# Embedding gathers that skip out-of-range rows, with the skipped places filled by ScalarE

## The chip, the cores and the metric

The kernel runs on one core of a Trainium2 chip. The metric is device time in microseconds (us). TensorE (PE) multiplies matrices, VectorE (DVE) and ScalarE (ACT) do elementwise work, GpSimd (POOL) here issues the gathers, and SyncE (SP) issues loads. PEld is TensorE's weight load, which runs beside its matmuls.

## The reference

A click-prediction network over 2048 samples. Each sample has 13 continuous and 26 categorical fields.

```python
cont_emb = emb_table[:CONT_FIELD][None, :, :] * conts[:, :, None]
cate_emb = emb_table[cates]                      # table: 12500 rows x 64 float32
cc = jnp.concatenate([cont_emb, cate_emb], axis=1)
pairs = jnp.einsum('bfd,bgd->bfg', cc, cc)[:, ROWS, COLS]
X = jnp.concatenate([cont_emb.reshape(B, -1), cate_emb.reshape(B, -1), pairs], axis=1)
X = relu(layernorm(X @ W1 + b1) * g + b)         # 1024 wide
X = relu(layernorm(X @ W2 + b2) * g + b)         # 1024 wide
return sigmoid(X @ Wout + bout)
```

The categories are drawn from ranges of up to about 100,000, but the table has 12,500 rows. An index at or beyond 12,500 reads the last row. In these inputs that is so for 37,651 of the 53,248 indices (71%): five fields never go beyond the table, and each of the other 21 does so in about 7 of 8 samples. So of the 128 rows of one gather 37.5 are ordinary rows on average.

## The kernel before

The batch is worked in 16 tiles of 128 samples. A tile passes through these steps:

- **Gather.** `gather(x, par)` (L474 to L485) on POOL issues 26 indirect DMAs (L481), one per categorical field. Each brings 128 rows of 256 bytes into a 64-column slice of `xb`. There is one `xb`, so tile x+1 is gathered into the places that tile x has left. The fields go in four groups, g0 to g3, of 8, 6, 6 and 6 gathers. Ahead of a group POOL waits on `trans_ready` until PE has transposed the same group of the tile before. In the loop, `progress` adds waits on older events of PE.
- **Transpose and split.** PE transposes a group (`transpose_group`, L540) into PSUM. ACT rounds it to the high part `x_hl[0]` (`split_group`, L759) and signals `ts_hi`; DVE subtracts to get the low part (L1061). Each float32 product is three matmuls (L516 to L518) of such parts.
- **Pair products.** ACT and DVE copy the parts into `g_still` and `g_move` (L765, L770, L1068). PE multiplies them in four fills, "gram 0" to "gram 3" (L583). ACT and DVE take the fills out (L800, L801, L1146, L1147), and the third fill has to wait until the first is taken.
- **First layer.** PE's order for a tile is written out by hand (`STEADY`): "own 1" to "own 3" are the transposes of groups g1 to g3 of this tile and "next 0" that of g0 of the next, with the 19 k-tiles of W1 and the four fills between them. DVE and ACT normalise the sums and store them (L748).
- **Second layer.** It starts after tile 15 and uses no gathers.

Every engine runs its instructions in the order in which they are written. In the first 90 us, W1 (some 10 MB) is loaded and split into high and low parts by ACT (L825) and DVE (L1080) beside the first two tiles. DVE turns the categories into indices in `index_chain`, which clamps them to 0 .. 12499, and copies a tile's 26 indices to `idx` two tiles ahead (`indices`, L992). One more indirect DMA (L450) brings 13 rows of 4096 bytes as padding.

Of the kernel before, what the change touches and what calls it, by code (L numbers as in the profile page):

```python
# [31 lines left out]
I32 = mybir.dt.int32  # L32
U32 = mybir.dt.uint32
ALU = mybir.AluOpType
ACT = mybir.ActivationFunctionType

P = 128
BATCH = 2048
TILES = BATCH // P
CONT = 13  # L40
CATE = 26
FIELDS = CONT + CATE
DIM = 64
VOCAB = 12500
# [22 lines left out]
GROUPS = ((0, 4), (4, 7), (7, 10), (10, 13))  # L67
NG = len(GROUPS)
# [66 lines left out]
def build(nc, conts, cates, emb, W1, b1, g1, be1, W2, b2, g2, be2, Wout, bout, rows, out):  # L135
    h1_dram = nc.dram_tensor("h1_scratch", (P, TILES, HID), F32, kind="Internal").ap()

    with ExitStack() as memory:
        def sb(name, shape, dt=F32, ctx=memory):
            return ctx.enter_context(nc.sbuf_tensor(name, shape, dt))  # L140

        def sem(name):
            return memory.enter_context(nc.semaphore(name))
# [31 lines left out]
        conts_sb = sb("conts_sb", [P, TILES * CONT])  # L175
        c1 = sb("c1", [P, CONT])
        idx_all = sb("idx_all", [P, TILES * CATE], U32)
        idx = sb("idx", [P, 2, CATE], U32)
        rows_sb = sb("rows_sb", [P, FK], U32)
        ee_bc = sb("ee_bc", [P, NN])  # L180
        ident = sb("ident", [P, P])
        small = sb("small", [P, 4 * 4])
        bn = small[:, 0:12].rearrange("p (h s) -> p h s", h=2)
        mv = small[:, 12:14]
        bout_bc = small[:, 14:15]
        st = sb("st", [P, 8])
        logit = sb("logit", [P, TILES])
        prob = sb("prob", [P, TILES])
        g1_col = sb("g1_col", [P, K2])
        be1_col = sb("be1_col", [P, K2])  # L190

# [39 lines left out]
        conts_in = sem("conts_in")  # L231
        e13_in = sem("e13_in")
        rows_in = sem("rows_in")
        idx_step = sem("idx_step")
        idx_done = sem("idx_done")
        ident_ready = sem("ident_ready")
# [73 lines left out]
        def stands_alone(eng):  # L310


            eng.sem_inc(passed, 1)

        def t_bank(g):

            return (tr[:, 0, :], gr[:, 1, :])[g % 2]
# [123 lines left out]
        @block.gpsimd  # L441
        def _(pool):
            nc.gpsimd.memset(ident[:, :], 0.0).then_inc(ident_ready, 1)
            pool.wait_ge(ident_ready, 1)
            nc.gpsimd.affine_select(out=ident[:, :], in_=ident[:, :], compare_op=ALU.not_equal, fill=1.0,
                                    base=0, pattern=[[-1, P]], channel_multiplier=1).then_inc(ident_ready, 1)

            def rows_under_zeros():

                nc.gpsimd.indirect_dma_start(  # L450
                    out=raw_lo[EK + FT][PART:PART_PAD, :], out_offset=None, in_=W1,
                    in_offset=bass.IndirectOffsetOnAxis(ap=rows_sb[0:PART_PAD - PART, 0:1], axis=0),
                ).then_inc(w1_pad, 16)

            def progress(x, f):

                if f == 7:
                    pool.wait_ge(f_trans, x - 1)
                    stands_alone(pool)
                elif f == 10:  # L460
                    pool.wait_ge(l_trans, x - 1)
                    stands_alone(pool)
                elif f == 14:
                    pool.wait_ge(trans_ready, NG * x)
                    stands_alone(pool)
                elif f in (21, 23, 25):
                    pool.wait_ge(gram_ready, FILLS * (x - 1) + (f - 19) // 2)
                    stands_alone(pool)

            def gather(x, par, first=False, tied=False):  # L470

                pool.wait_ge(idx_done, x + 1)
                stands_alone(pool)
                for g, (a, b) in enumerate(GROUPS):  # L474
                    if not first:
                        pool.wait_ge(trans_ready, NG * (x - 1) + g + 1)
                        stands_alone(pool)
                    for f in range(2 * a, 2 * b):
                        if tied:
                            progress(x, f)  # L480
                        nc.gpsimd.indirect_dma_start(  # L481
                            out=xb[:, f * DIM:(f + 1) * DIM], out_offset=None, in_=emb,
                            in_offset=bass.IndirectOffsetOnAxis(
                                ap=idx[:, par, f:f + 1], axis=0),
                        ).then_inc(gathered[g], 16)  # L485

            gather(0, 0, first=True)
            gather(1, 1)
            pool.wait_ge(rows_in, 16)
            rows_under_zeros()  # L490
            with pool.Fori(0, (TILES - 2) // 2) as i:
                for u in range(2):
                    gather(2 * i + (2 + u), u, tied=True)

            def affine2(x, par):

                pool.wait_ge(n2_ready, x + 1)
                if not isinstance(x, int) or x >= 2:
                    pool.wait_ge(logit_done, x - 1)
                nc.gpsimd.tensor_tensor(a2[par][:, :], n2[par][:, :], g2_bc, ALU.mult).then_inc(a2_mul, 1)  # L500
                pool.wait_ge(a2_mul, x + 1)
                nc.gpsimd.tensor_tensor(a2[par][:, :], a2[par][:, :], be2_bc, ALU.add).then_inc(a2_ready, 1)

            pool.wait_ge(par_in, 16 * 4)
            for x in range(2):
                affine2(x, x)
            with pool.Fori(0, (TILES - 4) // 2) as i:
                for u in range(2):
                    affine2(2 * i + (2 + u), u)
# [232 lines left out]
        def _(act):  # L742
# [5 lines left out]
                act.dma_start(h1_dram[:, at(x), :].rearrange("p o n -> p (o n)"), h1_row[:, :]).then_inc(h1_out, 16)  # L748

            act.dma_start(cates_sb, cates.rearrange("(p x) f -> p (x f)", x=TILES)).then_inc(cates_in, 16)  # L750
            act.dma_start(rows_sb[:, :], rows.bitcast(U32)).then_inc(rows_in, 16)
            act.dma_start(conts_sb[:, :], conts.rearrange("(p x) f -> p (x f)", x=TILES)).then_inc(conts_in, 16)

            def split_group(x, g):

                a, b = GROUPS[g]
                n = (b - a) * P
                act.wait_ge(trans_ready, NG * x + g + 1)
                nc.scalar.copy(x_hl[:, 0, a:b, :].rearrange("p k b -> p (k b)"), t_bank(g)[:, 0:n]).then_inc(ts_hi, 1)  # L759

            def still_copies(x, n):

# [211 lines left out]
        def _(dve):  # L974
# [23 lines left out]
            def index_chain(n, a, b, to, count=idx_step):  # L998

                f, s = cates_f[:, a:b], shift[:, a:b]  # L1000
                nc.vector.tensor_copy(f, cates_sb[:, a:b]).then_inc(idx_step, 1)
                dve.wait_ge(idx_step, n + 1)
                TS(s, f, 0.0, float(VOCAB), ALU.is_lt, ALU.mult).then_inc(idx_step, 1)
                dve.wait_ge(idx_step, n + 2)
                TT(f, f, s, ALU.add).then_inc(idx_step, 1)
                dve.wait_ge(idx_step, n + 3)
                TS(to.bitcast(I32), f, 0.0, float(VOCAB - 1), ALU.max, ALU.min).then_inc(count, 1)

            index_chain(0, 0, CATE, idx[:, 0, :], idx_done)
            index_chain(3, CATE, TILES * CATE, idx_all[:, CATE:TILES * CATE])  # L1010
            indices(1, 1)
            step(nc.vector.memset(parts[:, 128:192], 0.0))
            step(nc.vector.memset(vbd[:, :, :], 0.0))
            step(nc.vector.memset(ones, 1.0))
# [389 lines left out]
```

## Time and profile before

| | us |
|---|---|
| median of 3 runs | 801.86 |
| lowest and highest | 799.72, 802.04 |
| span of the profiled execution | 797.8 |
| median less that span | 4.1 |
| PE busy | 742.0 |
| DVE busy | 552.8 |
| ACT busy | 501.8 |
| POOL busy | 492.0 |

The profile gives the span from the first to the last instruction of one execution; a time of that execution by the clock of the runs isn't given, so the difference between the median and the span stands for what lies around it. The engines overlap, so busy times don't add up. The share of a busy time says little alone: POOL has nothing to issue in the second layer, so its gathers all lie in the first 560 us.

### The profile page before, as it was taken

The numbers are of one execution on the slowest core, as the hardware profiler recorded it, in microseconds if no ns is written. First come the engines' busy times: TensorE is split into PE (matmuls) and PEld (weight loads), VectorE is DVE, ScalarE is ACT, GpSimd is POOL, SyncE is SP. The second block draws the span as 40 slices with busy tenths as digits, with TensorE's granted clock in tenths as the row PEclk, the third lists the DMA queues.
The fourth block names the chain that finished last, engine by engine and source line by source line (L and its number), as shares of the span: only waits on it lengthen the run. The fifth ranks groups of instructions, "written<-read, shape, count | busy, mean of one in ns | idle before, by whom it ended". The sixth has DMA issues, their size and how long they took to land. (4 is left out here: it accounts for less than half of the span.)

```text
span 797.8 us, 11844 instructions
## 1 busy us (share of the span) xinstructions
PE 742.0 (93%) x3583; PEld 596.2 (75%) x3583; DVE 552.8 (69%) x1703; ACT 501.8 (63%) x878; POOL 492.0 (62%) x451
## 2 busy tenths in 40 slices
PE   5678889999999999999999999999799999999995
PEld 1446668787787877878788777787678888888884
DVE  7248677787776867777677776777577555665568
ACT  2386767777577775877757777686667455355451
POOL 6776777777777777777777777777000334334432
PEclk9889999999999999999999999999899999999998
DMA  9999584766748677485775867657465111011000
GB/s 278 185 172 119 36 52 25 54 49 29 50 27 53 48 28 50 26 53 49 28 49 26 49 53 27 48 27 51 103 199 205 28 53 53 26 53 53 26 1 1
DMA packets 26232, 50.69 MB, mean 64 GB/s; under 512 B 10413, under 2 KB 10669, under 8 KB 26208
## 3 DMA queue, kind: packets, MB, share of 16 engines
q0 software_dynamic: 13344, 13.71, 43.3%
q1 hardware_dynamic: 10128, 27.97, 10.8%
q10 hardware_dynamic: 2736, 8.71, 2.7%
q8 instruction: 12, 0.20, 0.1%
q14 instruction: 12, 0.10, 0.0%
HBM read 41.96 MB, written 8.40 MB: 63 GB/s over the span
## 5 line engine op out<-in xcount | busy, mean ns | idle before, releaser
L481 POOL DMA_INDIRECT xb<-in_L_rec_emb_table,idx x416 | 423.4, 1018 | 133.3 <-issue 124.6
L516 PE MATMUL acc<-w_hi,x_hl 128*128 128x512 f32 x416 | 176.1, 423 | 6.0 <-DVE x_hl L1061 4.0
L518 PE MATMUL acc<-w_hi,x_hl 128*128 128x512 f32 x416 | 166.7, 401 | 0.0
L517 PE MATMUL acc<-w_lo,x_hl 128*128 128x512 f32 x416 | 165.8, 399 | 0.0
L500 POOL TENSOR_TENSOR raw_lo<-raw_lo,raw_hi 128x1024 f32<-128x1024 f32 x14 | 33.4, 2388 | 154.9 <-ACT raw_lo L947 154.9
L770 ACT CAST g_move<-x_hl 64x384 fp32r<-64x384 f32 (+1 forms) x192 | 125.7, 655 | 2.8
L765 ACT CAST g_still<-x_hl 64x384 fp32r<-64x384 f32 (+1 forms) x96 | 100.6, 1048 | 1.9
L516 PE MATMUL acc<-w_hi 128*128 128x512 f32 x256 | 101.0, 394 | 0.0
L518 PE MATMUL acc<-w_hi,w_lo 128*128 128x512 f32 x256 | 99.9, 390 | 0.0
L516 PEld LDWEIGHTS acc<-w_hi,x_hl 128*128 128x128 f32 x416 | 80.7, 194 | 25.5 <-DVE x_hl L1061 5.7
L517 PE MATMUL acc<-w_lo,w_hi 128*128 128x512 f32 x256 | 99.7, 390 | 0.0
L518 PEld LDWEIGHTS acc<-w_hi,x_hl 128*128 128x128 f32 x416 | 80.0, 192 | 18.4
L517 PEld LDWEIGHTS acc<-w_lo,x_hl 128*128 128x128 f32 x416 | 80.9, 195 | 12.5
L516 PE MATMUL acc<-w_hi,f_slots 128*128 128x512 f32 x192 | 77.8, 405 | 4.2 <-DVE w_lo L1080 3.7
L518 PE MATMUL acc<-w_hi,f_slots 128*128 128x512 f32 x192 | 75.8, 395 | 0.0
L517 PE MATMUL acc<-w_lo,f_slots 128*128 128x512 f32 x192 | 75.5, 393 | 0.0
L1301 DVE TENSOR_TENSOR w_lo<-raw_lo,w_hi 128x256 fp32r<-128x256 f32 x64 | 34.6, 555 | 50.8 <-ACT w_hi L939 50.7
L1068 DVE TENSOR_SCALAR g_still<-x_hl 64x384 fp32r<-64x384 f32 (+1 forms) x96 | 66.0, 687 | 1.9
L1061 DVE TENSOR_TENSOR x_hl<-tr,x_hl 128x512 fp32r<-128x512 f32 (+1 forms) x32 | 20.0, 624 | 54.7 <-ACT x_hl L759 54.7
L518 PEld LDWEIGHTS acc<-w_hi,w_lo 128*128 128x128 f32 x256 | 48.1, 188 | 10.0
L516 PEld LDWEIGHTS acc<-w_hi 128*128 128x128 f32 x256 | 48.1, 188 | 9.5
L517 PEld LDWEIGHTS acc<-w_lo,w_hi 128*128 128x128 f32 x256 | 48.2, 188 | 9.4
(117 smaller groups left out, 1171.1 us busy)
## 6 DMA issues: line engine op xcount, KB each, us to landing
raw_lo<-in_L_rec_W SPq DMA_DIRECT2D x26, 512.0 KB, 9.4
h_scratch<-h_row ACTq DMA_DIRECT2D x16, 512.0 KB, 4.8
raw_hi<-h_scratch SPq DMA_DIRECT2D x16, 512.0 KB, 3.6
xb<-in_L_rec_emb_table,idx POOLq DMA_INDIRECT x416, 6.3
raw_hi<-in_L_rec_W SPq DMA_DIRECT2D x6, 512.0 KB, 7.2
raw_hi<-in_L_rec_b SPq DMA_DIRECT2D x1, 512.0 KB, 3.8
raw_hi<-in_L_rec_ln_g SPq DMA_DIRECT2D x1, 512.0 KB, 4.7
raw_hi<-in_L_rec_ln_b SPq DMA_DIRECT2D x1, 512.0 KB, 5.5
```

Source lines behind the costliest of these rows:

```text
L481: nc.gpsimd.indirect_dma_start(out=xb[:, f * DIM:(f + 1) * DIM], out_offset=None, in_=emb, in_offset=bass.IndirectOffsetOnAxis(ap=idx[:, p ...
L500: nc.gpsimd.tensor_tensor(a2[par][:, :], n2[par][:, :], g2_bc, ALU.mult).then_inc(a2_mul, 1)
L516: nc.tensor.matmul(o, a, w, start=first, stop=False)
L517: nc.tensor.matmul(o, a, v, start=False, stop=False)
L518: return nc.tensor.matmul(o, b, w, start=False, stop=last)
L765: nc.scalar.copy(*still_part(0, n, of))
L770: last = nc.scalar.copy(*move_part(n, m // 2, m % 2))
L1061: TT(x_hl[:, 1, a:b, :].rearrange("p k b -> p (k b)"), t_bank(g)[:, 0:n], x_hl[:, 0, a:b, :].rearrange("p k b -> p (k b)").bitcast(F32), A ...
L1068: last = TS(to, x_lo.bitcast(F32), 2.0, None, ALU.mult)
L1301: TT(y_lo[:, par, part, :], y[:, part, :], y_hi[:, par, part, :].bitcast(F32), ALU.subtract).then_inc(y_split, 1)
```

## The change

DVE clamps the indices to 12500 in place of 12499, so an index beyond the table becomes 12500. Each gather gets `bounds_check=VOCAB - 1` (12499) and `oob_is_err=False`: rows with an index above that are not to be written. What then stands in their place has been put there before: ACT copies the table's last row, which it has loaded once with 128 copies (`last_row`), over the whole place of a group (`fill`). It does so for all four groups at the start, and after that for group g right behind the rounding copy of group g, when the transpose has read the place. POOL now waits on `filled` in place of `trans_ready`. The first gather too waits on it.

To make room, `idx` becomes the first 52 columns of `idx_all` (so the copy of tile 1's indices goes), and `logit` and `prob` use `conts_sb`.

```diff
-        idx = sb("idx", [P, 2, CATE], U32)
+        idx = idx_all[:, 0:2 * CATE].rearrange("p (x f) -> p x f", x=2)
+        last_row = sb("last_row", [P, DIM])
-        logit = sb("logit", [P, TILES])
-        prob = sb("prob", [P, TILES])
+        logit, prob = conts_sb[:, 0:TILES], conts_sb[:, TILES:2 * TILES]
...
                 for g, (a, b) in enumerate(GROUPS):
-                    if not first:
-                        pool.wait_ge(trans_ready, NG * (x - 1) + g + 1)
-                        stands_alone(pool)
+                    pool.wait_ge(filled, NG * x + g + 1)
+                    stands_alone(pool)
...
                                 ap=idx[:, par, f:f + 1], axis=0),
+                            bounds_check=VOCAB - 1, oob_is_err=False,
                         ).then_inc(gathered[g], 16)
...
             act.dma_start(cates_sb, cates.rearrange("(p x) f -> p (x f)", x=TILES)).then_inc(cates_in, 16)
+            act.dma_start(last_row[:, :], emb[VOCAB - 1:VOCAB, :].to_broadcast([P, DIM])).then_inc(last_row_in, 16)
             act.dma_start(rows_sb[:, :], rows.bitcast(U32)).then_inc(rows_in, 16)
...
-            def split_group(x, g):
+            def fill(g):
+
+                a, b = GROUPS[g]
+                to = xb[:, 2 * a * DIM:2 * b * DIM].rearrange("p (f d) -> p f d", d=DIM)
+                nc.scalar.copy(to, last_row[:, :].unsqueeze(1).to_broadcast([P, 2 * (b - a), DIM])).then_inc(filled, 1)
+
+            def split_group(x, g, last=False):
...
                 nc.scalar.copy(x_hl[:, 0, a:b, :].rearrange("p k b -> p (k b)"), t_bank(g)[:, 0:n]).then_inc(ts_hi, 1)
+                if not last:
+                    fill(g)
+
+            act.wait_ge(last_row_in, 16)
+            for g in range(NG):
+                fill(g)
...
-                TS(to.bitcast(I32), f, 0.0, float(VOCAB - 1), ALU.max, ALU.min).then_inc(count, 1)
+                TS(to.bitcast(I32), f, 0.0, float(VOCAB), ALU.max, ALU.min).then_inc(count, 1)
...
-            indices(1, 1)
+            dve.wait_ge(idx_step, 7)
+            dve.sem_inc(idx_done, 1)
```

No call passes `last=True`, so tile 15's groups are followed by a fill too. On ACT, in the loop over the tiles, the stretch from g2's rounding copy (`x_hl<-tr`) to g3's (`x_hl<-gr`) reads like this before:

```order
L759 CAST x_hl<-tr 128x384
L787 CAST f_slots<-gr 128x384
L770 COPY g_move<-x_hl 64x7x128
L792 CAST f_slots<-gr 59x128
L770 COPY g_move<-x_hl 64x7x128
L758 REGISTER_ALU
L759 CAST x_hl<-gr 128x384
```

and like this after, on the same engine at the same place:

```order
L768 CAST x_hl<-tr 128x384
L761 COPY xb<-last_row 128x384
L802 CAST f_slots<-gr 128x384
L785 COPY g_move<-x_hl 64x7x128
L807 CAST f_slots<-gr 59x128
L785 COPY g_move<-x_hl 64x7x128
L767 REGISTER_ALU
L768 CAST x_hl<-gr 128x384
L761 COPY xb<-last_row 128x384
```

A fill stands behind each rounding copy, so everything that ACT does after it for the tile comes one fill later. At the start of ACT's program, ahead of W1's first rounding copy, stand now one more load and four fills:

```order
L752 DMA spare<-in_r_cates 128x416
L753 DMA last_row<-in_L_rec_emb_table 128x64
L754 DMA rows_sb<-feature_rows 128x1
L755 DMA conts_sb<-in_r_conts 128x208
L761 ACT_TABLE_LOAD
L761 COPY xb<-last_row 128x512
L761 COPY xb<-last_row 128x384 x3
L840 CAST w_hi<-raw_lo 128x1024 x4
```

The order of POOL's gathers and of PE's and DVE's work is as before.

## Rows read from the trace of the kernel before

**Rows 1.** The page: busy us, share of the span, instructions.
```profile
span 797.8 us, 11844 instructions
...
PE 742.0 (93%) x3583; PEld 596.2 (75%) x3583; DVE 552.8 (69%) x1703; ACT 501.8 (63%) x878; POOL 492.0 (62%) x451
```

**Rows 2.** The gathers' line L481: durations, POOL's idle time ahead of them, landing.
```profile
L481 POOL DMA_INDIRECT xb<-in_L_rec_emb_table,idx x416: 940/944/4307, 5.0 to 558.5; - x139
...
  issue: 124.6, 398
...
DMA to landing us min/median/max: 4.8/6.3/13.6
```

**Rows 3.** The page, part 5: count | busy, mean ns | idle before.
```profile
L481 POOL DMA_INDIRECT xb<-in_L_rec_emb_table,idx x416 | 423.4, 1018 | 133.3 <-issue 124.6
```

**Rows 4.** Timeline, POOL: start us, us, instruction [idle before]: first gather, three places, last.
```profile
5.02 1.32 POOL L481 DMA_INDIRECT xb<-in_L_rec_emb_table,idx  x1 [3.54 <-DVE idx L1007]
...
163.32 1.64 POOL L481 DMA_INDIRECT xb<-in_L_rec_emb_table,idx  x1 [0.30 <-issue]
...
186.50 0.95 POOL L481 DMA_INDIRECT xb<-in_L_rec_emb_table,idx  x1 [0.30 <-issue]
...
536.99 1.15 POOL L481 DMA_INDIRECT xb<-in_L_rec_emb_table,idx  x1 [0.30 <-issue]
...
558.49 0.94 POOL L481 DMA_INDIRECT xb<-in_L_rec_emb_table,idx  x1 [0.30 <-issue]
```

**Rows 5.** Timeline, PE: transposes of groups of tiles 4 to 7, then the last.
```profile
180.20 0.63 PE L540 MATMUL tr<-ident,xb 128*128 128x128 f32 x4 [0.33 <-DVE cc_dots L1147]
...
193.43 0.49 PE L540 MATMUL gr<-ident,xb 128*128 128x128 f32 x3
...
279.53 0.63 PE L540 MATMUL tr<-ident,xb 128*128 128x128 f32 x4 [0.32 <-DVE cc_dots L1147]
...
566.58 0.90 PE L540 MATMUL gr<-ident,xb 128*128 128x128 f32 x3 [4.28 <-DMA xb<-in_L_rec_emb_table,idx]
```

**Rows 6.** Waits from 100 to 570 us: total us, times, longest.
```profile
PEld gr L583 <- ACT cc_dots L801: 9.1, 14, 2.2
PE gr L540 <- DMA xb<-in_L_rec_emb_table,idx: 8.1, 5, 4.3
```

**Rows 7.** Timeline, POOL: its shortest instruction, its compare-and-select, and the padding gather.
```profile
0.25 0.10 POOL L1392 MEMSET const-float32-0.0<- 128x1 f32 x1 [0.25 <-issue]
...
1.19 0.29 POOL L445 TENSOR_SCALAR_AFFINE_SELECT ident<-ident 128x128 f32<-128x128 f32 x1 [0.24 <-POOL ident L443]
...
81.92 0.89 POOL L450 DMA_INDIRECT raw_lo<-in_L_rec_W,rows_sb  x1 [0.30 <-issue]
```

**Rows 8.** Timeline, ACT: tile 4 from g0's rounding copy to g3's.
```profile
180.87 0.59 ACT L759 CAST x_hl<-tr 128x512 fp32r<-128x512 f32 x1 [0.82 <-PE tr L540]
...
184.26 0.48 ACT L759 CAST x_hl<-gr 128x384 fp32r<-128x384 f32 x1 [2.80 <-PE gr L540]
184.77 3.69 ACT L765 CAST g_still<-x_hl 64x896 fp32r<-64x896 f32 x2
188.70 0.48 ACT L782 CAST f_slots<-tr 128x384 fp32r<-128x384 f32 x1 [0.24 <-PE tr L554]
...
194.08 0.48 ACT L759 CAST x_hl<-gr 128x384 fp32r<-128x384 f32 x1
```

**Rows 9.** Source L770, ACT's copies of 64x384 and 64x896: durations in ns.
```profile
L770 ACT CAST g_move<-x_hl x192: 507/513/947, 41.6 to 574.4; 64x384 fp32r<-64x384 f32 x128, 64x896 fp32r<-64x896 f32 x64
```

**Rows 10.** DMA from 20 to 60 us: share of the 16 engines by queue; landing.
```profile
q0 software_dynamic: 839, 0.87, 51.9%
q1 hardware_dynamic: 1717, 6.24, 46.4%
...
xb<-in_L_rec_emb_table,idx POOLq DMA_INDIRECT x29, 11.5
```

**Rows 11.** Windows: stretch, its us, busy (x instructions) of PE, PEld, DVE, ACT, POOL.
```profile
0.00:80.00 80.00, 56.38 (x193) 34.11 (x194) 46.46 (x132) 41.57 (x57) 57.23 (x58) 0.89 0.96 188
```

More of the change, by code:

```diff
@@ L233, in build @@
         rows_in = sem("rows_in")
+        last_row_in = sem("last_row_in")
+        filled = sem("filled")
         idx_step = sem("idx_step")
```

## The prediction

> **What bounds the kernel now.** I read the busy times first [rows 1]. PE is busy for 742.0 of 797.8 us, so it looks like the bound, with 56 us idle. POOL, at 62%, looks like an engine with room. The reader should not stop there. I then took the gathers' own line [rows 2, 3]: 416 gathers are busy for 423.4 us, and POOL is idle for 133.3 us ahead of them, of which 124.6 us is "issue", in 398 pieces of 0.31 us. That is time in which POOL waits for no other engine. So POOL runs one gather after another without a pause from 5.02 to 559.4 us [rows 4]: 423.4 + 133.3 + 5.0, less the 3.5 us of idle time ahead of the first, plus 1.2 for the padding gather, is 559.4. A usual gather takes 0.944 us and its gap 0.31, so 1.25 us, or 32.6 us for a tile's 26.
>
> The third thing to see is that this stream and PE are nearly equal in speed. From the first gather of g1 of tile 4 at 163.32 to that of tile 15 at 536.99 is 373.7 us for 11 tiles, 33.97 us each [rows 4]. PE, left alone, needs less: from the g0 transpose at 180.20 to that at 279.53 it does 3 tiles in 33.1 us each [rows 5]. The difference first eats up a lead: tile 4's last group is transposed at 193.43 without waiting. Later PE waits for the rows themselves, 8.1 us in five pieces, the last of 4.28 us at 566.58 [rows 5, 6]. So the first 567 us are set by the gather stream, with PE's own chain less than 1 us per tile behind it. What follows, 797.8 - 566.6 = 231 us, has no gathers, and I take it as unchanged. A nanosecond more per gather is then 0.42 us of the end. That is the most important number here.
>
> **The change, part by part.**
>
> The gather instruction itself. It gets a comparison for each of its 128 indices and some way to leave rows out. No row of the trace shows a gather with such a bound, so its price has to be bounded from both sides.
> Below: 71% of the rows, 91 of 128, are left out. If a row's share of the instruction is 0.944/128 = 7.4 ns and a row left out costs nothing, a gather is 0.67 us shorter [rows 2]. Against this end stands the padding gather: it has 13 rows (of 4096 bytes) in place of 128 and takes 0.89 us [rows 7]. By that row, leaving out 91 rows saves 91/115 x 0.055 = 0.04 us.
> Above: if a row left out has to be treated apart, and costs a row's share twice over, a gather is 0.67 us longer, +280 us for 416.
> Between them lie POOL's simple passes. Its shortest instruction over 128 lanes takes 0.10 us, and a compare-and-select over 128x128 takes 0.29 us [rows 7].
> I take +0.10 us. Work over 128 indices that is one more pass on the same engine is nearest to that row, and the saving by the padding row (0.04) is smaller than one pass. 416 x 0.10 = +41.6 us, all on the stream that sets the end, since POOL never waits for another engine. Both ends stay in the range.
>
> The Trainium skill, page "DMA: Bandwidth & Descriptors", section "Anatomy of one DMA — SWDGE (gpsimd) path", gives descriptor generation as "small, variable", with many descriptors before the cost shows. By it, the number of rows left out and the check would both hardly move a gather, and the sum would be that of rival 1 below. The padding row (0.89 against 0.94) agrees about the number of rows and is silent on the check. The same page, "SWDGE vs HWDGE vs iDMA", says that this path computes its descriptors in software, which speaks for a check that costs time in the gather.
>
> The transfers. The rows not moved relieve the DMA engines. The gathers' queue holds 51.9% of them from 20 to 60 us, when W1's loads hold 46.4% and a gather needs 11.5 us to land [rows 10]. Over the whole kernel the median is 6.3 us and the least 4.8 [rows 2]. At the end of the stream one landing counts once: 6.3 - 4.8 = -1.5 us. At the start, quicker landings let PE begin its first tiles up to some 5 us sooner (11.5 against 6.3), but POOL's stream does not move by that, and while it sets the end PE only waits longer afterwards. So this is 0 in my forecast and shows only where POOL becomes quicker.
>
> The fills on ACT. ACT's copies of 384 columns take 0.51 us and those of 896 take 0.95 [rows 9], about 0.86 ns per column and 0.18 fixed. A fill of 384 is then 0.51, one of 512 is 0.62, together 2.2 us per tile and 35 us over 16 tiles. What of it delays something? The fill of g0 lies in ACT's idle time ahead of g1 (2.80 us). The fill of g1 moves the 3.69 us of `g_still` copies by 0.51, of which ACT's wait of 0.24 ahead of the copy at 188.70 takes back a part: +0.24 remains at that place (188.94) [rows 8]. Then ACT has no idle time up to g3's rounding copy at 194.08, so the fill of g2 adds its 0.5: g3's split comes some 0.7 us later. DVE waits for it, its chain leads without a pause to the take-out of fill 1, and on that PE's third fill waits already now, 9.1 us in 14 pieces [rows 6]. So PE's own tile becomes 33.1 + 0.7 = 33.8 us. That still lies under the stream's 33.97. The fills cost nothing as long as POOL's gathers are not shorter, and up to 12 x 0.7 = 8.4 us if that cover goes. The fill behind g3 of tile 15 is not hidden: up to +0.5 us.
>
> The waits on `filled`. Queued behind each are all the later gathers. Tile 4's g0 is transposed at 180.20 and rounded from 180.87 on, so that with 0.6 for the copy and 0.6 for the fill `filled` comes at 182.1; POOL gets to that place at 186.50 [rows 4, 5, 8]. No stall there, and later tiles leave more room, since POOL falls back against PE. The first fill needs the last row to land and ACT's table to be loaded. I put +0.3 us on the first gather.
>
> The smaller edits: the index copy of tile 1 goes (0.2 us of DVE ahead of work that isn't waited for), clamping to 12500 costs the same, and the shared buffers are not used at the same time. 0.
>
> Sum: 797.8 + 41.6 - 1.5 + 0.5 + 0.3 = 838.7 us of span. With the 4.1 us by which the median lies above the span: 842.8 us, +5%.
>
> **The rivals.**
>
> 1. The gather takes the same time (within 5 ns). For it: its duration hardly depends on the number of rows [rows 7], and a comparison may be there already for every gather. Then the stream stays at 33.97 us per tile, the end moves by -1.5 + 0.5 + 0.3, and the time is 801.9 - 0.7 = 801 us. That would also be the time if rows beyond the bound were still moved (to nowhere, say), with landings as before: 802.
>
> 2. The gather becomes much dearer: each row left out is a case of its own for POOL, between 2 and 7.4 ns more. For it: 71% of the rows are such cases. Per gather 0.2 to 0.67 us, so +83 to +280 us; the middle, +0.4 us, gives 802 + 166 = 968 us. Against it: the padding row suggests that rows are handled in bulk.
>
> 3. Faster. The gather becomes shorter by anything between 0.04 and 0.67 us, because what isn't described isn't paid for. Then POOL is no bound, and PE's chain of 33.8 us per tile, stretched by the fills, sets the end. Against today's 33.97 that is 12 x 0.17 = -2 us. The rest comes from the start: PE is busy for only 56.4 of the first 80 us [rows 11], and earlier rows and W1 give back 5 to 15 of the other 24. This gives 802 - 2 - 10 = 790 us, and at best 785. It decides from a gather 0.01 us shorter on, since PE is less than 1 us per tile behind. So even a large saving on POOL is worth 2% at most.
>
> **How the numbers follow.** My forecast, a gather longer by 0.02 to 0.2 us, has 0.38: 842.8 us, with a range of its own from 809 to 884. Rival 2 has 0.25, rival 1 has 0.19, rival 3 has 0.18. About 0.3% (2.4 us) is what a measurement of this kernel can tell from no change. Faster by more: 0.16 from rival 3 and 0.03 from rival 1, 0.19. Within: 0.15 from rival 1 and 0.02 from rival 3, 0.17. Slower by more: 0.64. The 8-in-10 range leaves out the lower part of rival 3 (0.09) and the upper part of rival 2 (0.11, from +0.45 us per gather on): 790 to 990 us.
>
> **What would show it.** The duration of the gathers' line decides nearly all. A median near 1.04 us, POOL idle only for "issue", a tile every 36 to 37 us, and PE waiting for gathered rows in each tile: my forecast. A median of 0.944: rival 1. Over 1.15: rival 2, with durations that differ between the five fields without any index beyond the table and the 21 others. Under 0.93, no wait of PE for gathered rows, and ACT's copies as what PE waits for: rival 3. That rows are really skipped shows in the bytes of the gathers' queue (13.7 MB before, 4 MB expected) and in shorter landings. If ACT's fills take over 0.8 us, or POOL is seen waiting on them, the part on the fills was wrong. My forecast is wrong above all if one pass over the indices is not what the check costs.

## The result and the profile after

| | before | after |
|---|---|---|
| median of 4 runs | 800.79 | 815.10 |
| lowest and highest | 797.64, 802.04 | 814.46, 815.61 |
| span of the profiled execution | 797.8 | 813.3 |
| last group transposed | 566.58 | 582.75 |
| from there to the end | 231.2 | 230.6 |

The change makes the kernel slower: the ratio is 1.0184, interval [1.0147, 1.0221]. The second layer takes what it took, so all of the loss lies ahead of the last transpose.

The page of after answers to [rows 1 and 3] and shows what the gathers' queue moved:

```profile
span 813.3 us, 12347 instructions
...
PE 748.0 (92%) x3583; PEld 600.0 (74%) x3583; DVE 555.3 (68%) x1702; ACT 530.2 (65%) x946; POOL 516.0 (63%) x451
...
q0 software_dynamic: 13344, 4.22, 2.8%
...
L482 POOL DMA_INDIRECT xb<-in_L_rec_emb_table,idx_all x416 | 446.7, 1074 | 131.2 <-issue 122.5
```

The same queue on the page of before:

```profile
q0 software_dynamic: 13344, 13.71, 43.3%
```

The skipping works: q0 moved 4.22 MB where it moved 13.71 before, and its share of the 16 DMA engines over the span fell from 43.3% to 2.8%. It still counts 13,344 packets, 32 for each of the 417 gathers (the padding gather included), so this count doesn't follow the rows. POOL's gathers grew from 423.4 to 446.7 us and it still idles almost only for "issue".

The gathers' own line, as in [rows 2], which is L482 now (min/median/max in ns, then idle time ahead, then landing):

```profile
L482 POOL DMA_INDIRECT xb<-in_L_rec_emb_table,idx_all x416: 992/997/2220, 6.2 to 580.2; - x139
...
  issue: 122.5, 402
  ACT xb L761: 5.0, 2
...
DMA to landing us min/median/max: 2.2/2.4/6.4
```

The shortest gather went from 0.940 to 0.992 us and the median from 0.944 to 0.997: +0.053 us. From tile 3 on the shortest gather of each of the 26 fields takes 0.99 to 1.00 us, of those with skipped rows and of the five without alike. The landing fell from 6.3 to 2.4 us. POOL waited for ACT's fills twice, 5.0 us in all, 4.7 of it ahead of the first gather.

The timeline of POOL in after: the first gather, the first of g1 of tile 4, the last gather (as [rows 4]). Then PE's last transpose (as [rows 5]):

```profile
6.23 1.18 POOL L482 DMA_INDIRECT xb<-in_L_rec_emb_table,idx_all  x1 [4.74 <-ACT xb L761]
...
165.77 1.18 POOL L482 DMA_INDIRECT xb<-in_L_rec_emb_table,idx_all  x1 [0.30 <-issue]
...
580.23 1.00 POOL L482 DMA_INDIRECT xb<-in_L_rec_emb_table,idx_all  x1 [0.30 <-issue]
```

```profile
582.75 0.55 PE L542 MATMUL gr<-ident,xb 128*128 128x128 f32 x3 [2.64 <-DMA xb<-in_L_rec_emb_table,idx_all]
```

The stream ended at 559.4 before and ends at 581.2 now, +21.8 us: 416 x 0.053 = 22.0, +1.2 for the first gather (5.02 to 6.23), and -1.4 that is left over. Behind the stream's end PE transposed the last group after 7.2 us before (566.58 - 559.43) and after 1.5 us now (582.75 - 581.23), -5.6. That is +16.2 at the last transpose; the rest of the kernel is 0.7 shorter; +15.5 on the span.

Waits in after from 100 to 590 us, up to and with the last transpose, the same two kinds as [rows 6] (total us, times, longest):

```profile
PE gr L542 <- DMA xb<-in_L_rec_emb_table,idx_all: 20.9, 11, 2.6
...
PEld gr L585 <- ACT cc_dots L816: 7.2, 9, 2.2
```

PE waits 20.9 us for gathered rows where it waited 8.1. It seems to have won at the start: in the first 80 us it is busy for 59.7 us against 56.4 [rows 11], and W1's loads land after 5.4 us (9.4 before). Tile 3's g0 is transposed 2.6 us earlier (144.08 against 146.71; a second trace of before, `e14_before_third`, has it at 151.16). Nothing of that reaches the end. A consumer that is early waits for a stream that is late.

### The profile page after: what moved, and what is told of

The parts are those of the page before. It is cut to its first block and busy times, and to the rows that moved or that the text cites. A ratio compares the mean times of both kernels' runs of the same rounds, so it can differ in the third digit from the quotient of the medians.

```text
span 813.3 us, 12347 instructions
## 1 busy us (share of the span) xinstructions
PE 748.0 (92%) x3583; PEld 600.0 (74%) x3583; DVE 555.3 (68%) x1702; ACT 530.2 (65%) x946; POOL 516.0 (63%) x451
## 3 DMA queue, kind: packets, MB, share of 16 engines
q0 software_dynamic: 13344, 4.22, 2.8%
## 5 line engine op out<-in xcount | busy, mean ns | idle before, releaser
L482 POOL DMA_INDIRECT xb<-in_L_rec_emb_table,idx_all x416 | 446.7, 1074 | 131.2 <-issue 122.5
L518 PE MATMUL acc<-w_hi,f_slots 128*128 128x512 f32 x192 | 79.1, 412 | 4.3 <-DVE w_lo L1096 3.8
L520 PE MATMUL acc<-w_hi,f_slots 128*128 128x512 f32 x192 | 76.6, 399 | 0.0
```

Of the source, the lines that this page charges most:

```text
L482: nc.gpsimd.indirect_dma_start(out=xb[:, f * DIM:(f + 1) * DIM], out_offset=None, in_=emb, in_offset=bass.IndirectOffsetOnAxis(ap=idx[:, p ...
L518: nc.tensor.matmul(o, a, w, start=first, stop=False)
L520: return nc.tensor.matmul(o, b, w, start=False, stop=last)
```

## The experiments

**Which part of the change costs.** Three kernels do one part each. `e1_check_only` gives the gathers of before the bound, with all indices below it. `e2_skip_no_fill` is the kernel after, without ACT's fills behind the first four. `e3_fill_only` has all fills and no bound. The core of each edit, first of e1 against before:

```diff
                                 ap=idx[:, par, f:f + 1], axis=0),
+                            bounds_check=VOCAB - 1, oob_is_err=False,
```

e2 against after (POOL waits on `trans_ready` again, except for tile 0):

```diff
-                if not last:
-                    fill(g)
```

e3 against after:

```diff
-                            bounds_check=VOCAB - 1, oob_is_err=False,
...
-                TS(to.bitcast(I32), f, 0.0, float(VOCAB), ALU.max, ALU.min).then_inc(count, 1)
+                TS(to.bitcast(I32), f, 0.0, float(VOCAB - 1), ALU.max, ALU.min).then_inc(count, 1)
```

> The kernel before with the bound (12499) given to each gather, and one to the padding gather of 13 rows too. Indices are still clamped to 12499, so no row is left out; no fills; POOL waits on the transposes as before. The result is that of the reference. Theory (the check is a fixed price in every gather, whatever it leaves out): the gathers' median goes from 0.944 to 0.997 us as in the changed kernel, landings stay at 6.3 us as before, and the time is 801 + 416 x 0.053 = 823 us, more than the changed kernel's 815. If the price belongs to each index, the padding gather with its 13 indices grows by 0.005 us, if it belongs to the instruction, by 0.05. Rival (leaving rows out is what costs, the check alone is free): gathers stay at 0.944 us and the time at 801.

> The changed kernel without the fills of each tile: only the four at the start are left, and POOL waits on the transposes again from the second tile on. Left out of the computation: a skipped row keeps what stood in its place, so the output isn't the reference's. Theory (the fills are hidden behind the gather stream): gathers at 0.997 us and 1.3 us per step of the stream, time 814 to 815 us, the same as the changed kernel. Rival (ACT's 35 us of fills delay PE or POOL): clearly less, 805 to 810 us, down to 801 + 22 - 4 - ... if they were the whole loss.

> The changed kernel without the bound: indices are clamped to 12499 again, all rows are moved, and the fills and the waits on them stay. The result is that of the reference. Theory: gathers back at 0.944 us, landings at 6.3 us, the fills hidden apart from the first gather, which starts 1.2 us later as in the changed kernel: 802 to 803 us. Rival (the fills are part of the 14 us): 806 to 815 us.

Measured, against 801.34 us for the kernel before on that chip: e1 822.7 us, ratio 1.0232 [1.0164, 1.0301]; e2 816.33, 1.0166 [1.0105, 1.0227]; e3 801.12, 0.9981 [0.9948, 1.0013]. The gathers' line in e1, then in e3:

```profile
L482 POOL DMA_INDIRECT xb<-in_L_rec_emb_table,idx x416: 991/997/2468, 5.2 to 583.6; - x139
...
DMA to landing us min/median/max: 2.4/5.5/13.1
```

```profile
L482 POOL DMA_INDIRECT xb<-in_L_rec_emb_table,idx_all x416: 938/944/2242, 6.2 to 557.7; - x139
```

The bound alone lengthens a gather by the full 0.053 us, with nothing skipped and nothing filled. So the skipping is free in itself, and it pays for a part of its check: e1 is 6 us slower than e2 on the same chip. In the two traces the last transposes are 9.1 us apart (590.74 in e1, 581.66 in e2). Of that, 5.7 us is the stream's end (584.6 and 578.9), which differs between executions though the gathers' median is the same. The other 3.4 us lies behind it: 6.2 us in e1, 2.8 in e2. The last transpose in e1 (timeline of PE):

```profile
590.74 0.90 PE L542 MATMUL gr<-ident,xb 128*128 128x128 f32 x3 [6.04 <-DMA xb<-in_L_rec_emb_table,idx]
```

The padding gather of e1 doesn't decide between a price of the index and one of the instruction, as was expected of it: it took 1.60 us, but 1.59 in after too, where it has no bound.

The fills cost nothing that can be measured, with the stream above them (e2 against after) or at its old speed (e3). But in e3 they used up the margin. PE's third fill waits longer, and PE no longer waits for gathered rows (waits from 100 to 575 us, before and then e3):

```profile
PE gr L583 <- ACT cc_dots L801: 3.5, 6, 2.0
```

```profile
PE gr L584 <- ACT cc_dots L815: 8.7, 14, 2.0
```

**What makes the landings long.** In before, 91 rows of a gather are on average one and the same row of the table (112 in 21 fields, none in five). `e4_spread_rows` moves all 128 rows of every gather, but spread over the table.

```diff
-                TS(to.bitcast(I32), f, 0.0, float(VOCAB - 1), ALU.max, ALU.min).then_inc(count, 1)
+                TS(to.bitcast(I32), f, 0.12, float(VOCAB - 1), ALU.mult, ALU.min).then_inc(count, 1)
```

> The kernel before with other data: each index is 0.12 times the category, so that the rows of a gather are spread over the table where 91 of 128 were the same last row before. As many rows and bytes are moved, no bound is given. Changed in the computation: other rows of the table are read, so the output isn't the reference's. Theory (what made a landing 6.3 us is that most rows of a gather are one and the same row in memory): landings fall to 2.5 to 3.5 us with gathers at 0.944, and the time by that difference, once, to 797 or 798 us. Rival (it is the number of rows moved): landings stay near 6.3 us and the time at 801.

It ran in 794.97 us, 0.9892 [0.9828, 0.9955], 2 to 3 us below what was expected. Its page shows the queue, its gathers' line the landing:

```profile
q0 software_dynamic: 13344, 13.71, 9.0%
```

```profile
L481 POOL DMA_INDIRECT xb<-in_L_rec_emb_table,idx x416: 940/944/3176, 5.1 to 558.9; - x139
...
DMA to landing us min/median/max: 2.3/2.4/6.2
```

It moves the 13.71 MB of before, yet takes 9.0% of the engines in place of 43.3%, and lands in 2.4 us in place of 6.3. So the skipped bytes were never the cost. The repeated row was, and this kernel gets the benefit of after's landings without its check (on other data, so it is no replacement). Why a repeated row takes the engines longer, no run shows. How closely the gathers follow one another seems to matter too: the median landing is 5.5 us in e1, with 0.053 us more from one gather to the next, and 3.9 in e5 below, with 20 gathers a tile. Its last transpose comes at 562.35, 2.5 us behind the stream's end. The Trainium skill, page "DMA: Bandwidth & Descriptors", section "Anatomy of one DMA — SWDGE (gpsimd) path", puts a DMA on this path at about 2.0 us plus bytes over 436 GB/s. By that page, an estimate for these 32 KB is 2.1 us. The trace of e4 agrees within 0.3 us (2.4); that of before, with the same bytes, doesn't (6.3).

**What a fill costs without its cover.** `e5_fewer_gathers` leaves out 6 of a tile's 26 gathers from tile 2 on, so POOL is no bound. `e6_fewer_gathers_fill` is that with all of ACT's fills.

```diff
+LEFT_OUT = (5, 6, 7, 13, 19, 25)
...
+                        if not first and f in LEFT_OUT:
+                            continue
...
-                pe.wait_ge(gathered[g], n * x + n)
+                m = n - 16 * sum(2 * a <= f < 2 * b for f in LEFT_OUT)
+                pe.wait_ge(gathered[g], m * x + n)
```

> The kernel before with 6 of the 26 gathers of each tile left out from the second tile on (fields 5, 6, 7, 13, 19 and 25; their places keep the first tile's rows, so this part of the computation is left out and the output isn't the reference's). No bound, no fills. It takes POOL's stream off the path: 20 x 1.25 = 25 us per tile against PE's 33.1. Theory (the stream sets the first 567 us, and PE's own chain is 0.5 to 1 us per tile behind it): PE waits for no gathered row, a tile takes 33.1 us, time 801 - (4 for the last landing, 4 to 8 for the tiles) = 789 to 793 us. Rival (PE is the bound already, and POOL's stream only happens to be as long): 799 to 801 us.

> The same with the fills and with POOL waiting on them, still without the bound. Left out as in the run without fills. Theory (the fills are hidden only by the gather stream; without that cover each costs what it delays g3's split by, 0.7 us per tile, so 0.6 to 0.8 x 12 and 0.5 at the end): PE waits longer for the third fill of the pair products, and the time is 7 to 10 us above that of the run without fills, 797 to 802 us. Rival (ACT has idle time enough): within 2 us of it.

Against 802.23 us: e5 795.32, 0.9908 [0.9871, 0.9946]; e6 801.8, 0.9998 [0.9966, 1.003]. The last transposes (timelines of PE, e5 and then e6) have no wait ahead of them:

```profile
561.13 0.49 PE L544 MATMUL gr<-ident,xb 128*128 128x128 f32 x3
```

```profile
568.35 0.49 PE L545 MATMUL gr<-ident,xb 128*128 128x128 f32 x3
```

e5's time lies above the 789 to 793 us expected, though its tiles take what was expected: between tile 3's g0 and tile 15's, PE takes 33.16 us per tile (149.97 to 547.84), and 33.50 in e6 (153.09 to 555.10). A tile's fills thus cost PE 0.35 us, about 4 us over 12 tiles. The two traces are 3 us apart at tile 3 already, no more than two traces of before (146.71 and 151.16), so these 3 aren't shown to be the fills'. By the medians the fills cost 6.5 us. That is nearly all that a free POOL wins here (6.9 us, e5), so a free POOL with the fills is worth nothing against before (0.9998).

**What the check costs by itself.** `e7_probes` adds 20 gathers after tile 15, each waiting for the one before: four each of 13 rows, 13 rows with the bound, 128 rows, 128 rows with the bound, and 128 rows with bound 0, which leaves out nearly all.

```diff
+            for rows, bound in ((13, None), (13, VOCAB - 1), (P, None), (P, VOCAB - 1), (P, 0)):
+                for again in range(4):
...
+                        in_offset=bass.IndirectOffsetOnAxis(ap=idx_all[0:rows, 60:61], axis=0), **more,
```

> The kernel before with the changed kernel's shared buffers, and 20 gathers more on POOL between its last gather and the second layer, where it has nothing to do: four each of 13 rows without a bound, 13 rows with a bound that none exceeds, 128 rows without, 128 rows with that bound, and 128 rows with the bound 0, beyond which nearly all rows lie. Each waits until the one ahead has landed. The result is that of the reference. What is measured is the shortest duration of each kind. Theory A (the check is a fixed price of the instruction): +0.05 us at 13 rows as at 128, and nothing more or less for rows left out. Theory B (it is paid per index): +0.005 us at 13 rows and +0.05 at 128. Under both the time stays at 801 us.

The time, 810.29 us in one execution, missed the expectation of no change: the probes ran until 644 us and held up POOL's own work in the second layer. Their durations are what counts. The shortest of the four, in that order: 0.87, 0.92, 0.94, 1.00, 0.99 us. POOL's timeline, a probe of 13 rows with the bound, one of 128 with it, and one that leaves nearly all out:

```profile
580.77 0.92 POOL L503 DMA_INDIRECT last_row<-in_L_rec_emb_table,idx_all  x1 [3.64 <-DMA last_row<-in_L_rec_emb_table,idx_all]
...
621.72 1.00 POOL L503 DMA_INDIRECT last_row<-in_L_rec_emb_table,idx_all  x1 [3.22 <-DMA last_row<-in_L_rec_emb_table,idx_all]
...
639.45 0.99 POOL L503 DMA_INDIRECT last_row<-in_L_rec_emb_table,idx_all  x1 [1.40 <-DMA last_row<-in_L_rec_emb_table,idx_all]
```

The bound adds 0.05 us with 13 rows and 0.05 to 0.06 with 128. It is a price of the instruction and not of its indices. On POOL's queue a register MOVE of 29 ns stands ahead of each gather with the bound 12499. It isn't the price: the four probes with bound 0 have none and take as long. Rows cost little (115 more rows: 0.07 us), and leaving them out saves 0.01 at most.

**Only where it could help.** If a landing counts only at the stream's end, the skipping is wanted for the last group alone. `e8_last_group_skips` gives the bound to the last six gathers of tile 15 and needs one fill. The loops' last turns are written out for it.

```diff
+                    more = dict(bounds_check=VOCAB - 1, oob_is_err=False) if last and g == NG - 1 else {}
...
-                                ap=idx[:, par, f:f + 1], axis=0),
+                                ap=idx[:, par, f:f + 1], axis=0), **more,
```

> A version that takes from the change only what pays: only the six gathers of tile 15's last group get the bound and skip rows, behind one fill of that group by ACT; all other gathers are as before. The result is that of the reference. Theory (the check costs 0.053 us in each gather with the bound, and quicker landings count once, at the end of the stream): +0.3 us of stream and up to 3.9 us less of landing, PE's wait ahead of the last transpose falls from 4.3 to under 1.5 us, time 797 to 799 us, ratio 0.995 to 0.998. Rival (the gathers ahead still read the one last row and hold the DMA engines, so that the last ones land as late as before): 801 us.

It took 802.45 us, 0.9995 [0.9962, 1.0029]: no gain. The trace does show what was wanted (timeline of PE):

```profile
566.67 0.49 PE L548 MATMUL gr<-ident,xb 128*128 128x128 f32 x3
```

The wait of 4.28 us is gone, yet the transpose comes when it came before. In this execution POOL started its last gather at 560.88, 2.4 us later than in the first trace of before (558.49). Another trace of before, `e14_before_third` below, has it at 562.13 and the last transpose at 570.05 with 4.38 us of waiting, on a span of 802.2. PE's own order comes last in e8: its transpose ahead of that one is at 563.16, against 558.61 and 561.98 in the two traces of before. So the stream's end and PE's place both wander by some 4 us from one execution to the next, as much as this edit could give. The interval leaves room for a gain of up to 0.4% and for none.

**Copies of the row.** e4 says that the last row should not be read 91 times. `e9_copies_of_the_row` makes a table of its own in DRAM, the 12,500 rows and 128 copies of the last one, behind W1's loads, and gathers from it from tile 4 on. An index beyond the table is spread over the copies by DVE.

```diff
+    table = nc.dram_tensor("table", (VOCAB + COPIES, DIM), F32, kind="Internal").ap()
...
+            sp.dma_start(table[VOCAB:VOCAB + COPIES, :],
+                         emb[VOCAB - 1:VOCAB, :].to_broadcast([COPIES, DIM])).then_inc(table_in, 16)
...
+                TS(s[:, own:], f[:, own:], 0.00125, float(VOCAB), ALU.mult, ALU.add).then_inc(count, 1)
+                dve.wait_ge(idx_step, n + 5)
+                TT(f[:, own:], f[:, own:], s[:, own:], ALU.min).then_inc(count, 1)
```

> A version that goes for the shorter landings without paying the check: after W1's last load, SyncE copies the table (3.2 MB) inside DRAM, with 128 copies of its last row behind it; from tile 4 on the gathers read that table, and an index beyond the table is turned into one of the 128 copies, spread by the category's value. All rows are moved, no bound, no fills. The result is that of the reference. Theory (a landing of 6.3 us comes from one row being read 91 times, and landings count once, at the end of the stream): gathers at 0.944 us, landings at 2.4 us from tile 4 on, time 801 - 4, plus up to 1 us for three more index operations at the start: 797 to 798 us, ratio 0.993 to 0.997. Rival (the copy inside DRAM delays W1's last tiles or the gathers of tiles 2 and 3, and gives it back): 800 us or more.

It took 804.96 us, 1.0029 [0.9999, 1.0059]. From tile 4 on the gathers land in 2.4 us, as wanted. But the copy of 3.2 MB in one piece took 24.3 us. Beside it the padding gather landed after 21.6 us (8.4 in before), POOL stood for 10.3 us, and PE waited for the last parts of W1 (waits of POOL and PE in e9). That the copy caused these waits is argued from their time alone:

```profile
POOL xb L491 <- issue: 131.4, 386, 10.3
...
PE acc L529 <- DVE w_lo L1102: 18.0, 4, 15.0
```

So the copy was cut into ten pieces, each released by one of PE's later events. `e10_copied_in_pieces` and `e11_pieces_again` took 940.46 and 929.89 us in comparisons in which the kernel before took 918 and 901 us; there they are 1.0287 [1.0228, 1.0346] and 1.0372 [1.0311, 1.0433] of it. `e12_before_again`, the kernel before beside e11 (901.26 us, 1.003 [0.999, 1.007]), shows why they say little of the question: POOL's waits on PE's transposes, 0.30 us each in before, last 2.2 us on average there (waits in e12), ACT's and DVE's waits on PE are longer too, and the gathers end at 652 us. The order by hand runs under other conditions there. What makes them so stays open: the record gives e12 and e16 below the same chip number, and beside e16 the kernel before took 801.12 us.

```profile
POOL xb L481 <- PE tr L540: 30.7, 14, 4.0
```

> The version with copies of the last row once more, with its one fault taken away: the table is copied in ten pieces of 320 KB, one behind each of the tiles 1 to 10, when the first tiles and W1 are over, and only tiles 12 to 15 gather from it. The result is that of the reference. Theory (the loss of the version before was the 3.2 MB copy at 74 us, behind which the padding gather took 21.6 us to land): the first 160 us are as in the kernel before, landings fall from 6.3 to 2.4 us from tile 12 on, and the last transpose comes up to 4 us sooner: 797 to 799 us, ratio 0.994 to 0.998. Rival (PE's own chain is as late as the stream in most executions, so that a landing 4 us shorter gives it nothing to do sooner): 801 us, ratio 0.998 to 1.002.

> The version with the table copied in ten pieces, unchanged, once more: its first comparison fell on a chip where the kernel before took 918 us, with waits of the engines on each other that no other run shows. Theory and rival as then: 797 to 799 us with a ratio of 0.994 to 0.998, or a ratio of 0.998 to 1.002.

> The kernel before, unchanged, for a second trace of it on the same chip. The time is that of before, 801 us. What is read is where PE stands when tile 15's last group is gathered. Theory A (the first trace is typical): PE comes to the last transpose at 562 us and waits some 4 us for rows. Theory B (the first trace is of a quick execution, since it lies 2 us under the median, and PE's chain is mostly as late as the stream): it comes at 565 us or later and waits under 1.5 us, which would explain why shorter landings of the last group alone changed nothing.

Where the kernel before took its usual time (802.98 us), `e13_pieces_third` switched at tile 12, with the kernel before beside it (`e14_before_third`), and with `e15_fewer_and_spread`, which is e5 and e4 together. The edits of e13 beside those of e9:

```diff
+OWN_TABLE = 12
+PIECES = 10
...
+            for piece in range(PIECES):
+                sp.wait_ge(acc_ready, 2 + piece)
```

> The version with the table copied in ten pieces, unchanged; its two comparisons so far fell on chips where the kernel before takes 900 us and more. Theory (what is gained is the last landing, up to 4 us): ratio 0.994 to 0.998. Rival (PE's chain is mostly as late as the stream, so the shorter landing gives nothing): 0.998 to 1.002.

> The kernel before, unchanged, for a second trace on a usual chip. Theory A (its first trace is typical): tile 3's g0 is transposed at 147 us, and PE waits some 4 us for the rows of tile 15's last group. Theory B (PE's chain is mostly as late as the stream, because the first tiles take a few us more in most executions): tile 3's g0 at 150 us or later, and a last wait under 1.5 us.

> The kernel before with both: 6 of the 26 gathers of a tile left out from the second tile on, and the rows of a gather spread over the table. Left out and changed as in the two runs that do one of these, so the output isn't the reference's. POOL's stream is off the path here, so landings can only count in the first tiles. Theory (shorter landings also bring the first tiles forward, beside the last landing): 2 to 6 us less than with the 6 gathers left out alone, 789 to 793 us, ratio 0.984 to 0.989. Rival (shorter landings count only at the end of the stream): the same as with the 6 gathers left out alone, 795 us, ratio 0.991.

e13 took 811.34 us, 1.0116 [1.0081, 1.015]: the last piece is released by an event of PE, POOL runs ahead of PE, and so it stood for 16.7 us at the switch. e14 took 802.73, 0.9996 [0.9961, 1.0031], as it should. Neither of its theories fits whole: tile 3's g0 comes at 151.16 as in B, and PE's last wait is 4.38 us as in A. e15 took 785.19, 0.9767 [0.9735, 0.98], 10 us less than e5 (different chips, each against its own runs of before), and more than the 2 to 6 expected. Tile 3's g0 is transposed at 142.81 there against 149.97 in e5: the short landings give some 7 us in the first tiles. The size rests on two traces, the direction on more: that transpose comes at 141.6 to 144.1 us in the four traces with short landings from the start (after, e2, e4, e15), and at 146.5 to 153.1 in those of before, e1, e3, e5 to e8, e13, e14 and e16. In after nothing of it reaches the end.

`e16_own_table_at_14` switches two tiles later, when all pieces have landed, and uses the short landings for tiles 14 and 15 only.

```diff
-OWN_TABLE = 12
+OWN_TABLE = 14
```

> The version with the table copied in ten pieces, with only tiles 14 and 15 gathering from it. With tile 12, POOL came to the copied table while the last piece was not there and stood for 16.7 us; two tiles later it has been there for long. The result is that of the reference. Theory (the end of the stream is where the shorter landing counts): POOL doesn't wait for the table, the last transpose comes under 3 us after the stream's end in place of 7.0 to 7.2, and the time is 2 to 4 us less than before, ratio 0.995 to 0.998. Rival (PE's own chain comes to the last transpose as late, and the copies cost the stream as much elsewhere): ratio 0.998 to 1.003.

It took 796.73 us where before took 801.12, 0.9936 [0.9909, 0.9963], and is faster than both kernels (0.6% below before). Its gathers' two lines, its landing from the copied table, and the last transpose, with no wait ahead of it:

```profile
L495 POOL DMA_INDIRECT xb<-in_L_rec_emb_table,idx x364: 940/944/3999, 5.1 to 489.5; - x182
L495 POOL DMA_INDIRECT xb<-table,idx x52: 940/944/2327, 490.8 to 557.6; - x52
```

```profile
xb<-table,idx POOLq DMA_INDIRECT x52, 2.4
```

```profile
564.35 0.49 PE L558 MATMUL gr<-ident,xb 128*128 128x128 f32 x3
```

The last transpose is 6.7 us behind the start of the last gather (557.63), against 8.1 in before and 7.9 in e14, and it waits for nothing. It is PE's own order now that comes last. So the transpose is 5.8 us behind the stream's end, not under 3 as expected, and these 1.2 to 1.4 us are a part only of the 4.4 us gained. The rest isn't located: the stream ends at 558.6 here, against 559.4 and 563.1 in the two traces of before.

## Why the prediction came out as it did

I forecast 842.8 us, and it is 815.1. The direction, the path and the place of the loss were right: POOL's stream, pause for pause, set the end, and the check went onto it 416 times. The time also lies in the range that I gave this case by itself (809 to 884). The size was nearly three times too large (+5.1% on the 801.86 us that I had, against +1.8%). Term by term, on the span:

| step | forecast | measured | by |
|---|---|---|---|
| the check, 416 times | +41.6 | +22.0 | 0.053 us each, after and e1 |
| landing at the stream's end | -1.5 | -5.6 | 7.2 us became 1.5 |
| first gather | +0.3 | +1.2 | timeline |
| last fill, second layer | +0.5 | -0.7 | 231.2 and 230.6 |
| rest of the stream | 0 | -1.4 | remainder |
| sum on the span | +40.9 | +15.5 | |
| median less span | 4.1 | 1.8 | 815.1 - 813.3 |

**The step that failed first** is "I take +0.10 us. Work over 128 indices that is one more pass on the same engine is nearest to that row." I took the check for work over the indices. e7 shows that it is paid once per instruction: 0.05 us with 13 rows and with 128. The padding gather hinted at this [rows 7]. With a tenth of the indices it took 94% of a gather's time, so most of a gather is fixed, and an option of it would most likely be fixed too. I used that row for the saving and not for the cost. It gave no size for the bound; e1 and e7 did. The term was +41.6 us and is +22.0, which is most of the miss.

**The second** is the landing: "At the end of the stream one landing counts once: 6.3 - 4.8." That is a difference between the median and the shortest landing of one kernel, and both stand under the repeated row. What counts is the time from the stream's end to the last transpose, and the trace of before had it: 566.58 - 559.43 = 7.2 us. I had not seen why landings were long. I put them down to W1's loads and to the number of rows, and neither holds for the last tile. e4 shows the cause, one row read 91 times by a gather on average. Even the shortest landing of before is 4.8 us, while the median of e4 is 2.4. With that known, about -5 us could have been reckoned for the term.

**The third** is the 4.1 us between median and span, and no step of the mechanism. Other profiled executions are 2.1 us longer by the clock of the runs than their span (815.36 and 813.3 in after; 804.3 and 802.2 in e14). By that, the one I worked from was an execution of about 799.9 us, 2 us quicker than the median, while the one profiled of after lies at its median. So the spans are 15.5 us apart and the medians 14.3.

**Right, and shown:** the fills are hidden (e2, e3), last 0.51 and 0.62 us (506 to 628 ns over 68 fills), and behind the first gather POOL waits for one of them, 0.3 us (after). Their price without cover I had at up to 8.4 + 0.5; it is 6.5 us (e6 against e5). That these are near each other is partly luck: PE's tile grew by 0.35 us and not by 0.7, and the other 2 to 3 us come from no term of mine. W1's quicker loads and the earlier first tiles are worth nothing while the stream sets the end (after). The padding row's reading that skipped rows save at most 0.04 us was right too: leaving out nearly all of 128 saved 0.01 (e7). The Trainium skill, page "DMA: Bandwidth & Descriptors", section "Anatomy of one DMA — SWDGE (gpsimd) path", calls descriptor generation "small, variable". The 0.07 us that 115 more rows take in e7 agree.

**The rivals.** Rival 1 (within 5 ns) is out by the median of 0.997. Rival 2 (each left-out row a case of its own) is out by e1, where no row is left out and the gather is as long. Rival 3 held that earlier rows give back 5 to 15 us at the start once POOL is no bound. That mechanism exists (some 7 us, e15 against e5), but it needed a shorter gather, and no run shows one that lasts under 0.94 us with 128 rows: bound 0 leaves out nearly everything and still takes 0.99 us.

## What to carry to other kernels

Where one engine issues hundreds of small DMAs without a pause, count per instruction: an option that costs 0.05 us costs 22 us here, and rows or bytes left out of each give that engine nothing back. Look at how far behind the stream's end its consumer is: that is what quicker landings shortened (7.2 us to 2.5 in e4, to 1.5 in after). And where landings are long, ask whether the rows are distinct before asking how many there are.

## What the runs showed of the hardware

- Gathers of which a part reads one 256-byte row (91 of 128 on average, none in five of the 26 fields) land in 6.3 us (median), those with rows spread over the table in 2.4. With 128 copies of the row in DRAM it is 2.4 too (e9, e16). The queue's share of the DMA engines is 43.3% against 9.0% for the same 13.71 MB and the same 13,344 packets (before, e4). With the repeated row's transfers gone, W1's 512 KB loads land in 5.4 us (after) or 5.7 (e4) in place of 9.4.
- A bound on a gather costs 0.05 us with 13 rows and with 128 (e7; 0.053 in after and e1). The gap between gathers stays at 0.30 us. Rows left out take 0.01 us at most off POOL's time (e7), and each gather counts 32 packets, with 13 rows or 128 and with rows left out or not.
- The unchanged kernel took 901 and 918 us in two sets of runs against 801 to 803 in the others. Its granted clock was 0.952 in the trace at 898 us and 0.980 in the first trace of before; PE was busy for 769 us against 742, so most of the difference is waiting. What causes it wasn't found.
